# Second attention: the 48 maxima of a step spread over its slots by a build-time table

## The chip, the cores and the metric

The kernel runs on one core of one Trainium2 chip. The core has a tensor engine (PE in the profile, with PEld for its weight loads), a vector engine (DVE), a scalar engine (ACT), a GpSimd engine (POOL) and a sync engine that issues DMAs (SP). The metric is the device time of one execution in microseconds (us); lower is better. Several runs are taken, and the median is compared. One more execution is profiled.

## The reference, cut to what matters

The kernel computes a layer of two residual blocks on `x` of shape (4, 1024, 256): an attention with 16 heads of 64, then a transformer block that holds a second, grouped attention and a mixture of experts. The change lies in the second attention alone, which has 16 query heads and 4 key-value heads of 16 columns:

```
scores = jnp.einsum('bqhd,bkhd->bhqk', q, k) * scale
scores = jnp.where(causal[None, None], scores, jnp.finfo(scores.dtype).min)
probs = jax.nn.softmax(scores, axis=-1)
attn = jnp.einsum('bqhk,bkhd->bqhd', probs, v)
```

(The last line stands for the product of the probabilities with the values.) The softmax takes the maximum of each row first. It is these maxima that the change moves.

## The kernel before, in words

`attention_two` (line 1103) goes through 16 tasks, one for each of 4 batches and 4 key-value heads, with 4 query heads each. Its `run` (line 1141) makes a pipeline of them: `step(n1, n2, n3)` prepares task n1 (stacks and maxima), computes scores, exponentials and outputs of task n2, and brings out the second half of task n3. So there are 16 steps with work on n1, then two more that drain.

Every engine goes through the same `NU2` = 48 slots `k` of a step, and the program writes down in each slot what that engine does there; nothing is reordered later. A slot has one unit of scores: `UNITS2[k]` is (c, j, h), queries of half c (512 of them), key tile j of 128, head h. Below the diagonal all 512 columns are computed, on it fewer. Slots 0 to 15 are c = 0 with 512, 384, 256 and 128 columns, four slots each; slots 16 to 35 have 512 columns, 36 to 47 again 384, 256 and 128.

In a slot PE does, in this order (`step`, lines 1390 to 1437): the scores of slot k (line 1332); at each fourth slot, for the two units that trail from the task before, an output group of four heads (line 1346); in slots 0, 3, 8, 12 and 16 a stack (line 1370), eight transposes that bring the keys or one head's queries into a PSUM bank; the maxima of the slot (line 1381); at each fourth slot, later ones, the output group; and in a few slots the turns: `turn_minus` (line 1387) transposes the negated maxima of a half, and `turn_out` (line 1352) the outputs. "Output group u" below is that of unit u of the current task; group 0 stands in slot 11, group 1 in slot 15, and so on every four slots up to group 9 in slot 47. The last two units of a task come in slots 3 and 7 of the next step.

A max is a matmul of 128 queries against up to 512 keys into one of three shared banks `b_MX`, which DVE then reduces to one column of `b_peak`. `MAX2[u]` says which. Where the key block holds the diagonal, `reduce_max` (line 1271) adds the causal mask and takes the maximum in one masked operation of 128 to 512 columns followed by a reading of its accumulator (line 1279); else it is a plain reduction of 512 columns (line 1282). Maxima 0 to 15 are all masked, with 128, 256, 384 and 512 columns in turn, four per head; they make the first half. From 16 on plain and masked ones alternate. Behind max 15 and max 47 DVE takes the negated maximum of the half (line 1288); PE transposes it, DVE splits it (lines 1296, 1298), and two DMAs of SP put it into two rows of `b_Q`, which scores 0 and 16 wait for.

Before the change max u stands in slot u + 6, one in every slot, so that maxima 42 to 47 ("late") fall into slots 0 to 5 of the next step, while the next task's stacks begin there. Max 4h, the first of head h, also waits for ACT's copies of the stacks (lines 1238, 1240) it reads. `share_banks` (line 1076) gives stacks, maxima and late maxima their banks in the order of the program: before, the stacks of slots 0, 8, 12 and 16 are in bank 0, that of slot 3 in bank 2, maxima 0 to 13 alternate between banks 1 and 2, and from 14 on they go round all three. A matmul into a bank waits until the last user has been read (`bank_free`).

Scores go round three banks of their own, `b_SC`: score k waits for the exponential of score k - 3 on ACT (line 1229). POOL zeroes the upper triangle of the probabilities (line 1171).

Of the kernel before, what the change touches and what calls it, by code (L numbers as in the profile page):

```python
# [16 lines left out]
P = 128  # L17
BANK = 512
# [19 lines left out]
def first_col(c, j):  # L38

    return max(0, j * P - c * BANK)  # L40
# [727 lines left out]
def project_two(nc, x, hold, w_qkv, ln1, cos2, sin2, norm_z, shift_z, V2, stack_dram):  # L768
# [3 lines left out]
    with ExitStack() as ctx:  # L772
# [251 lines left out]
        def _(pe):  # L1024
# [31 lines left out]
UNITS2 = [(c, j, h) for c, j in UNITS for h in range(GROUP)]  # L1056
NU2 = len(UNITS2)
MAX2 = [(h, i, c) for first in (True, False) for h in range(GROUP) for i, c in MAXU if (i < BANK // P) == first]
# [4 lines left out]
MAX_START = 6  # L1063
TAKE2 = (24, 8)
HALF_MAX = (16, NU2)
TURN_SLOTS = (MAX_START + 20, MAX_START + 3)
SCORE_BANKS, MAX_BANKS = 3, 3
OUT_SLOTS = (16 + LAG2 + 5, LAG2 + 3)
MAX_AT = {k: [n for n in range(NU2) if n + MAX_START == k] for k in range(MAX_START + NU2)}


SHARED = [x for k in range(NU2) for x in [("stack", n) for n, at in enumerate(STACK_SLOTS) if at == k]
          + [("max", u) for u in MAX_AT.get(k, ())] + [("late", u) for u in MAX_AT.get(k + NU2, ())]]

# [17 lines left out]
def used_so_far(n1, n2, x):  # L1092

    bank = SHARED_BANK[x]
    mine = [y[0] for y in SHARED[:SHARED.index(x)] if SHARED_BANK[y] == bank]
    if n2 is None:
        return LATE_USES[bank] + len(mine) - mine.count("late")
    if n1 is None:
        return (n2 + 1) * SHARED_USES[bank] + mine.count("late")
    return n1 * SHARED_USES[bank] + len(mine)  # L1100


def attention_two(nc, stack_dram, V2, A2):

    with ExitStack() as ctx:
# [141 lines left out]
        @block.vector  # L1247
        def _(dve):
            dve.memset(peak[:, :, :, :], 3 * NEG).then_inc(s["dve_consts"], 1)
            for i in range(2):  # L1250
                dve.memset(K[i][STACK:, :], 1.0).then_inc(s["dve_consts"], 1)
            dve.wait_ge(s["dve_consts"], 3)
            dve.wait_ge(s["consts"], 6)
            for b in range(MAX_BANKS):
                dve.sem_inc(bank_used[b], LATE_USES[b])
            dve.sem_inc(s["turn_copied"], 1)
            for c in range(2):
                dve.sem_inc(minus_in[c], 1)
            dve.sem_inc(s["A2_done"], 1)

            def rows_out(n2, c):
                b, g = n2 // KV2, n2 % KV2
                dve.wait_ge(s["OT_ready"], n2 * 2 + c + 3)
                O4 = SM[:, :].rearrange("p (t h w) -> p t h w", t=4, h=GROUP)
                dve.reciprocal(inv[:, c, :, :], O4[:, :, :, DH2]).then_inc(s["inv_ready"], 1)
                dve.wait_ge(s["inv_ready"], n2 * 2 + c + 1)
                dve.tensor_tensor(A2[:, bass.ds(b * ST_N + 4 * c, 4), bass.ds(g * (GROUP * DH2), GROUP * DH2)].rearrange(
                    "p t (h d) -> p t h d", h=GROUP), O4[:, :, :, 0:DH2],
                    inv[:, c, :, :].rearrange("p t (h a) -> p t h a", a=1).to_broadcast([P, 4, GROUP, DH2]), ALU.mult).then_inc(s["A2_done"], 1)

            def reduce_max(n, u, n1, n2, x):
                h, i, ch = MAX2[u]
                w = min(BANK, (i + 1) * P - ch * BANK)
                bank = SHARED_BANK[x]
                dve.wait_ge(s["max_ready"], n * NU2 + u + 1)
                if ch == i * P // BANK:

                    dve.sem_inc(s["due"], 1)
                    dve.tensor_tensor_reduce(MX[bank][:, 0:w], MX[bank][:, 0:w], causal[:, BANK - w:], 1.0, 3 * NEG,  # L1279
                                             ALU.add, ALU.max, peak[:, h, i, ch:ch + 1]).then_inc(bank_used[bank], 1)  # L1280
                else:
                    dve.tensor_reduce(peak[:, h, i, ch:ch + 1], MX[bank][:, 0:w], AX.X, ALU.max).then_inc(bank_used[bank], 1)  # L1282
                for c in range(2):
                    if u == HALF_MAX[c] - 1:
                        for b in range(MAX_BANKS):
                            y = [y for y in SHARED[:SHARED.index(x) + 1] if SHARED_BANK[y] == b and y[0] == x[0]][-1]
                            dve.wait_ge(bank_used[b], used_so_far(n1, n2, y) + 1)
                        dve.tensor_reduce(minus[c][:, :, :], peak[:, :, 4 * c:4 * c + 4, :], AX.X, ALU.max,
                                          negate=True).then_inc(s["minus_ready"], 1)

            def turn(n, c):
                dve.wait_ge(s["turn_ready"], n * 2 + c + 1)

                dve.wait_ge(minus_in[c], n * 32 + 1)
                T = SM[0:GROUP * ST_N // 2, 0:P]
                dve.tensor_copy(hi[c][:, :], T).then_inc(s["turn_copied"], 1)
                dve.wait_ge(s["turn_copied"], n * 4 + 2 * c + 2)
                dve.tensor_tensor(lo[c][:, :], T, hi[c][:, :], ALU.subtract).then_inc(s["turn_copied"], 1)

            def step(n1, n2, n3, p):  # L1300
                for k in range(NU2):
                    for c, m in ((0, n2), (1, n3)):
                        if m is not None and k == OUT_SLOTS[c] + 2:
                            rows_out(m, c)
                    for u in MAX_AT[k]:
                        if n1 is not None:
                            reduce_max(n1, u, n1, n2, ("max", u))
                    for u in MAX_AT.get(k + NU2, ()):
                        if n2 is not None:
                            reduce_max(n2, u, n1, n2, ("late", u))  # L1310
                    for c, m in ((0, n1), (1, n2)):
                        if m is not None and k == TURN_SLOTS[c]:
                            turn(m, c)

            run(dve, step)

        @block.tensor
        def _(pe):
# [71 lines left out]
            def step(n1, n2, n3, p):  # L1390
                for k in range(NU2):
                    unit = k // GROUP - TRAIL
                    last_head = k % GROUP == GROUP - 1
                    if n2 is not None and k > 0:
                        scores(n2, 1 - p, k)
                    if n3 is not None and last_head and unit < 0:
                        output(n3, p, NU + unit)
                    if n1 is not None and k in STACK_SLOTS:
                        n = STACK_SLOTS.index(k)
                        if n == 0:  # L1400
                            pe.wait_ge(loaded[p], (n1 - p) * 72 + 144)
                        stack(n1, n2, p, n)
                    for u in MAX_AT[k]:
                        if n1 is not None:
                            maximum(n1, p, u, n1, n2, ("max", u))
                    for u in MAX_AT.get(k + NU2, ()):
                        if n2 is not None:
                            maximum(n2, 1 - p, u, n1, n2, ("late", u))
                    if n2 is not None and k == 0:

                        scores(n2, 1 - p, 0)
                    if n2 is not None and last_head and unit >= 0:
                        output(n2, 1 - p, unit)
                    if n2 is not None and k == TURN_SLOTS[1]:
                        if n3 is not None:
                            rows_done(n3, 0)
                        else:
                            turned(n2, 0)
                        turn_minus(n2, 1)
                    if n3 is not None and k == OUT_SLOTS[1]:  # L1420
                        if n2 is not None:
                            turned(n2, 1)
                        else:
                            rows_done(n3, 0)
                        turn_out(n3, 1)
                    if n1 is not None and k == TURN_SLOTS[0]:
                        if n3 is not None:
                            rows_done(n3, 1)
                        elif n2 is not None:
                            turned(n2, 1)  # L1430
                        turn_minus(n1, 0)
                    if n2 is not None and k == OUT_SLOTS[0]:
                        if n1 is not None:
                            turned(n1, 0)
                        else:
                            rows_done(n3, 1)
                        turn_out(n2, 0)
# [773 lines left out]
```

## Time and profile before

| | us |
|---|---|
| median of 3 runs | 2751.97 |
| lowest and highest | 2751.84, 2753.37 |
| the profiled execution | 2745.91 |
| its span, first to last instruction | 2744.2 |
| PE busy | 2388.5 (87%) |
| DVE busy | 1636.8 (60%) |
| ACT busy | 1446.1 (53%) |
| POOL busy | 965.5 (35%) |

The span is one execution's; the profiled execution's own time is 1.7 us longer than it. Busy times count each engine's instructions alone. Matmuls are pipelined, so that the durations of neighbours overlap: the distance from start to start says what a matmul costs the next. The mean granted clock of PE over the span is 0.945 of full speed.

### The profile page before, as it was taken

What the parts mean: (1) busy time and instruction counts of PE and PEld (TensorE: products, weight loads), DVE (VectorE), ACT (ScalarE), POOL (GpSimd) and SP (SyncE); (2) the same over time, 40 slices, a digit from 0 to 9 for tenths busy, and PEclk for the clock granted to TensorE, in tenths of its full rate; (3) what the DMA queues carried; (4) which work ended last, traced back from release to release, by engine and by line L of the source; (5) the groups of instructions that cost most, each with busy time, mean ns of one, the idle gap of its engine ahead of it and who ended that gap; (6) DMA issues with size and microseconds to landing.
All of it is one profiled execution on the core that took longest, in us unless ns stands there. A gap on an engine that the chain in (4) does not pass through costs nothing. (4 is left out here: it accounts for less than half of the span.)

```text
span 2744.2 us, 45471 instructions
## 1 busy us (share of the span) xinstructions
PE 2388.5 (87%) x12594; PEld 1372.3 (50%) x12595; DVE 1636.8 (60%) x4291; ACT 1446.1 (53%) x3189; POOL 965.5 (35%) x1727
## 2 busy tenths in 40 slices
PE   4999999999999999999735899999998749999980
PEld 2555566555665556555512333333334626666650
DVE  5676664776467773676188777777773452222227
ACT  3566654666456663665257477777775412222222
POOL 0344433444345542444326122222222033333323
PEclk8999999999999999999968799999999869999995
DMA  3011110101001110111124111111111611111114
GB/s 103 17 28 29 25 44 15 29 22 41 24 19 29 29 44 14 29 26 28 32 97 194 40 35 34 35 35 35 35 34 58 218 51 44 46 44 46 46 55 163
DMA packets 134983, 135.01 MB, mean 49 GB/s; under 512 B 67840, under 2 KB 104448, under 8 KB 133120
## 3 DMA queue, kind: packets, MB, share of 16 engines
q1 hardware_dynamic: 125760, 109.58, 13.4%
q0 software_dynamic: 6912, 18.88, 2.1%
q10 hardware_dynamic: 2112, 4.19, 0.4%
q8 instruction: 88, 1.44, 0.2%
q14 instruction: 111, 0.91, 0.1%
HBM read 87.50 MB, written 33.82 MB: 44 GB/s over the span
## 5 line engine op out<-in xcount | busy, mean ns | idle before, releaser
L288 POOL TENSOR_TENSOR a_A<-a_A,a_P 128x512 f32<-128x512 f32 (+3 forms) x320 | 316.5, 989 | 289.8 <-PE a_O L594 279.0
L1229 ACT ACTIVATE b_P<-b_SC 128x512 f32<-128x512 f32 (+3 forms) x768 | 328.8, 497 | 163.0 <-PE b_SC L1332 161.4
L442 ACT ACTIVATE a_P<-a_SC 128x512 f32<-128x512 f32 (+3 forms) x640 | 292.0, 469 | 201.2 <-PE a_SC L577 194.9
L500 DVE CUSTOM_DVE_ANT_0 a_MX<-a_MX,a_causal 128x128 f32<-128x128 f32 (+3 forms) x512 | 248.5, 501 | 154.8 <-PE a_MX L646 149.3
L576 PE MATMUL a_SC<-a_QR,a_KR 128*128 128x512 f32 (+3 forms) x768 | 317.3, 417 | 4.6 <-DMA a_QS<-a_minusT 2.9
L1171 POOL TENSOR_SCALAR_AFFINE_SELECT b_P<-b_P 128x128 f32<-128x128 f32 x512 | 147.0, 294 | 443.0 <-ACT b_P L1229 433.6
L646 PE MATMUL a_MX<-a_KR,a_QR 128*128 128x512 f32 (+3 forms) x768 | 282.6, 377 | 17.5 <-DVE a_peak L500 14.3
L1279 DVE CUSTOM_DVE_ANT_0 b_MX<-b_MX,b_causal 128x128 f32<-128x128 f32 (+3 forms) x512 | 248.5, 498 | 80.3 <-PE b_MX L1381 78.1
L1381 PE MATMUL b_MX<-b_K,b_Q 96*128 96x512 bf16 (+3 forms) x768 | 251.7, 339 | 42.3 <-ACT b_Q L1240 14.0
L577 PE MATMUL a_SC<-a_QS,a_KS 65*128 65x512 f32 (+3 forms) x768 | 264.5, 348 | 0.0
L327 POOL TENSOR_SCALAR_AFFINE_SELECT a_P<-a_P 128x128 f32<-128x128 f32 x448 | 144.8, 329 | 339.7 <-ACT a_P L442 336.3
L1955 PE MATMUL e_GU<-W,e_hT 128*128 x576 | 261.8, 597 | 1.0 <-ACT e_hT L2007 0.8
L1332 PE MATMUL b_SC<-b_Q,b_K 98*128 98x512 bf16 (+3 forms) x768 | 245.5, 330 | 3.5 <-ACT b_P L1229 1.5
L594 PE MATMUL a_O<-a_P,a_V 128*64 128x512 f32 (+3 forms) x1280 | 232.6, 476 | 3.8 <-POOL a_P L327 3.8
L503 DVE TENSOR_REDUCE a_peak<-a_MX 128x1 f32<-128x512 f32 x256 | 169.7, 684 | 94.2 <-PE a_MX L646 94.1
L288 DVE TENSOR_TENSOR a_A<-a_A,a_P 128x512 f32<-128x512 f32 (+3 forms) x320 | 212.5, 664 | 16.6 <-PE a_O L594 6.1
L576 PEld LDWEIGHTS a_SC<-a_QR,a_KR 128*128 128x128 f32 x768 | 145.0, 189 | 148.1 <-issue 69.0
L1282 DVE TENSOR_REDUCE b_peak<-b_MX 128x1 f32<-128x512 f32 x256 | 176.0, 687 | 41.4 <-PE b_MX L1381 40.4
L620 PE MATMUL a_PK<-hold,a_W 128*128 128x512 f32 x384 | 187.2, 611 | 10.1 <-DMA a_W<-in_w_pair 6.8
L646 PEld LDWEIGHTS a_MX<-a_KR,a_QR 128*128 128x128 f32 x768 | 145.7, 190 | 85.8 <-DVE a_peak L500 55.3
L2047 DVE TENSOR_TENSOR e_gate<-e_gate,e_GU 128x512 f32<-128x512 f32 x72 | 49.5, 688 | 208.2 <-PE e_GU L1955 208.2
L1346 PE MATMUL b_O<-b_P,b_V 128*32 128x512 f32 (+3 forms) x1536 | 163.4, 498 | 0.2
(258 smaller groups left out, 4083.5 us busy)
## 6 DMA issues: line engine op xcount, KB each, us to landing
a_inv<-inv_rows SPq DMA_DIRECT2D x128, 128.0 KB, 3.1
stack_rows<-p_stk SPq DMA_DIRECT2D x32, 480.0 KB, 2.7
a_W<-in_w_pair SPq DMA_DIRECT2D x34, 384.0 KB, 3.9
b_stk<-stack_rows SPq DMA_DIRECT2D x136, 96.0 KB, 2.1
W<-in_w SPq DMA_DIRECT2D x8, 1024.0 KB, 5.5
n_x<-in_x SPq DMA_DIRECT2D x4, 1024.0 KB, 9.5
a_xT<-hold SPq DMA_DIRECT2D x4, 1024.0 KB, 4.9
a_fold<-a_total SPq DMA_DIRECT2D x256, 1.0 KB, 2.0
```

The costliest lines, as they stand in the source:

```text
L288: eng.tensor_tensor(acc[h][c][:, a:], acc[h][c][:, a:], buffer(n, h)[:, a:], ALU.add).then_inc(added[h], 1)
L442: act.activation(buffer(n, h)[:, a:], SC[h][:, a:], ACT.Exp, scale=DH1 ** -0.5).then_inc(s["exp_done"], 1)
L500: dve.tensor_tensor_reduce(MX[c % MAX_BANKS1][:, 0:w], MX[c % MAX_BANKS1][:, 0:w], causal[:, BANK - w:], 1.0, 3 * NEG, ALU.add, ALU.max, p ...
L576: pe.matmul(SC[h][:, a:], KR[p][h][:, keys], QR[p][h][:, queries], start=True, stop=False)
L577: pe.matmul(SC[h][:, a:], KS[p][h][:, keys], QS[p][h][:, queries], start=False, stop=True).then_inc(s["scores_ready"], 1)
L594: pe.matmul(O[DH1 * h:DH1 * (h + 1), a:], V[p][h][:, j, :], buffer(n, h)[:, a:], start=(j == 0), stop=(n in LAST)).then_inc(s["pv_done"], 1)
L646: pe.matmul(bank[:, 0:w], QR[p][h][:, i * P:(i + 1) * P], KR[p][h][:, ch * BANK:ch * BANK + w], start=True, stop=True).then_inc(s["max_rea ...
L1229: act.activation(probs[k % RING2][:, a:], SC[k % SCORE_BANKS][:, a:], ACT.Exp, scale=DH2 ** -0.5).then_inc(s["exp_done"], 1)
L1279: dve.tensor_tensor_reduce(MX[bank][:, 0:w], MX[bank][:, 0:w], causal[:, BANK - w:], 1.0, 3 * NEG, ALU.add, ALU.max, peak[:, h, i, ch:ch + ...
L1332: pe.matmul(SC[k % SCORE_BANKS][:, a:], K[p2][:, j * P:(j + 1) * P], Q[p2][:, c, h, a:], start=True, stop=True).then_inc(s["scores_ready"], 1)
L1381: last = pe.matmul(MX[SHARED_BANK[x]][:, 0:w], Q[p][0:STACK, i // 4, h, i % 4 * P:(i % 4 + 1) * P], K[p][0:STACK, ch * BANK:ch * BANK + w] ...
L1955: last = pe.matmul(GU[i][half][:, :], hT[i][:, kt, :], W13[:, bass.ds(e, 1), kt, half * FFN:(half + 1) * FFN].rearrange("p a f -> p (a f)" ...
```

## The change

`MAX_AT`, the table from slots to maxima, is no longer "max u in slot u + 6". `spread_maxima` gives each slot of PE a weight, its score columns + 300, and each max one for DVE, its columns + 150, and puts each next max into the first slot at which PE's share of the step has reached DVE's share of the maxima so far. The result, written out:

- slots with two maxima: 1 (43, 44), 6 (0, 1), 18 (12, 13), 22 (17, 18), 29 (25, 26), 31 (27, 28)
- slots with none: 5, 13, 30, 42, 44, 46
- in all others one, in the same order: max 2 in slot 7, max 8 in 14, max 19 in 23, max 29 in 32, max 37 in 40, max 41 in 47, max 47 in 4.

`TURN_SLOTS` is computed from the table and becomes (25, 8) instead of (26, 9). `share_banks` runs over the new order: the stacks of slots 0, 3 and 16 are now in bank 0, those of 8 and 12 in bank 1, and the late maxima alternate between 1 and 2. The rest of the diff lets the code cope with a slot without maxima and a bank without late ones.

```diff
--- before.py
+++ after.py
@@ -1063,10 +1063,28 @@
 MAX_START = 6
 TAKE2 = (24, 8)
 HALF_MAX = (16, NU2)
-TURN_SLOTS = (MAX_START + 20, MAX_START + 3)
 SCORE_BANKS, MAX_BANKS = 3, 3
 OUT_SLOTS = (16 + LAG2 + 5, LAG2 + 3)
-MAX_AT = {k: [n for n in range(NU2) if n + MAX_START == k] for k in range(MAX_START + NU2)}
+
+
+
+def spread_maxima():
+
+    pe = [BANK - first_col(c, j) + SLOT_COST for c, j, h in UNITS2]
+    dve = [(BANK if ch != i * P // BANK else (i + 1) * P - ch * BANK) + MAX_COST for h, i, ch in MAX2]
+    at, done, k = {}, 0, MAX_START
+    for u in range(NU2):
+        while sum(pe[m % NU2] for m in range(MAX_START, k + 1)) / sum(pe) < done / sum(dve):
+            k += 1
+        at.setdefault(k, []).append(u)
+        done += dve[u]
+    return at
+
+
+SLOT_COST, MAX_COST = 300, 150
+MAX_AT = spread_maxima()
+MAX_SLOT2 = {u: k for k, us in MAX_AT.items() for u in us}
+TURN_SLOTS = (MAX_SLOT2[HALF_MAX[0] - 1] + 5, MAX_SLOT2[NU2 - 1] + 4 - NU2)
 
 
 SHARED = [x for k in range(NU2) for x in [("stack", n) for n, at in enumerate(STACK_SLOTS) if at == k]
@@ -1252,7 +1270,8 @@
             dve.wait_ge(s["dve_consts"], 3)
             dve.wait_ge(s["consts"], 6)
             for b in range(MAX_BANKS):
-                dve.sem_inc(bank_used[b], LATE_USES[b])
+                if LATE_USES[b]:
+                    dve.sem_inc(bank_used[b], LATE_USES[b])
             dve.sem_inc(s["turn_copied"], 1)
             for c in range(2):
                 dve.sem_inc(minus_in[c], 1)
@@ -1283,8 +1302,9 @@
                 for c in range(2):
                     if u == HALF_MAX[c] - 1:
                         for b in range(MAX_BANKS):
-                            y = [y for y in SHARED[:SHARED.index(x) + 1] if SHARED_BANK[y] == b and y[0] == x[0]][-1]
-                            dve.wait_ge(bank_used[b], used_so_far(n1, n2, y) + 1)
+                            here = [y for y in SHARED if SHARED_BANK[y] == b]
+                            done = [y for y in here if y[0] == x[0] and SHARED.index(y) <= SHARED.index(x)]
+                            dve.wait_ge(bank_used[b], used_so_far(n1, n2, done[-1]) + 1 if done else used_so_far(n1, n2, here[0]))
                         dve.tensor_reduce(minus[c][:, :, :], peak[:, :, 4 * c:4 * c + 4, :], AX.X, ALU.max,
                                           negate=True).then_inc(s["minus_ready"], 1)
 
@@ -1302,7 +1322,7 @@
                     for c, m in ((0, n2), (1, n3)):
                         if m is not None and k == OUT_SLOTS[c] + 2:
                             rows_out(m, c)
-                    for u in MAX_AT[k]:
+                    for u in MAX_AT.get(k, ()):
                         if n1 is not None:
                             reduce_max(n1, u, n1, n2, ("max", u))
                     for u in MAX_AT.get(k + NU2, ()):
@@ -1400,7 +1420,7 @@
                         if n == 0:
                             pe.wait_ge(loaded[p], (n1 - p) * 72 + 144)
                         stack(n1, n2, p, n)
-                    for u in MAX_AT[k]:
+                    for u in MAX_AT.get(k, ()):
                         if n1 is not None:
                             maximum(n1, p, u, n1, n2, ("max", u))
                     for u in MAX_AT.get(k + NU2, ()):
```

Line numbers move by 20: scores are line 1352 in the changed kernel, outputs 1366, `turn_out` 1372, stacks 1390, maxima 1401, `turn_minus` 1407. The names are those of the banks and tiles: `b_SC` a score, `b_MX` a max or a stack, `b_O` an output group.

PE's instructions in slots 20 to 25 of a step with work on all three tasks, from max 15 to max 19. Before:

```order
L1381 MATMUL b_MX<-b_K,b_Q 128x512
L1332 MATMUL b_SC<-b_Q,b_K 128x512
L1381 MATMUL b_MX<-b_K,b_Q 128x512
L1332 MATMUL b_SC<-b_Q,b_K 128x512
L1381 MATMUL b_MX<-b_K,b_Q 128x128
L1346 MATMUL b_O<-b_P,b_V 32x128 x4
L1332 MATMUL b_SC<-b_Q,b_K 128x512
L1381 MATMUL b_MX<-b_K,b_Q 128x512
L1332 MATMUL b_SC<-b_Q,b_K 128x512
L1381 MATMUL b_MX<-b_K,b_Q 128x256
```

and now:

```order
L1401 MATMUL b_MX<-b_K,b_Q 128x512
L1352 MATMUL b_SC<-b_Q,b_K 128x512
L1401 MATMUL b_MX<-b_K,b_Q 128x512
L1352 MATMUL b_SC<-b_Q,b_K 128x512
L1401 MATMUL b_MX<-b_K,b_Q 128x128
L1401 MATMUL b_MX<-b_K,b_Q 128x512
L1352 MATMUL b_SC<-b_Q,b_K 128x512
L1401 MATMUL b_MX<-b_K,b_Q 128x256
L1366 MATMUL b_O<-b_P,b_V 32x128 x4
```

Max 18 (512 columns) now follows max 17 (128) at once, and max 19 (256) stands ahead of the output group (`b_O`) instead of two scores behind it.

PE's instructions in slots 10 to 12, from max 4 on. Before:

```order
L1381 MATMUL b_MX<-b_K,b_Q 128x128
L1332 MATMUL b_SC<-b_Q,b_K 128x256
L1381 MATMUL b_MX<-b_K,b_Q 128x256
L1346 MATMUL b_O<-b_P,b_V 32x512 x4
L1332 MATMUL b_SC<-b_Q,b_K 128x128
L1370 MATMUL b_MX<-b_identb,b_stk 96x128 x8
L1381 MATMUL b_MX<-b_K,b_Q 128x384
```

and now, from slot 9:

```order
L1401 MATMUL b_MX<-b_K,b_Q 128x128
L1352 MATMUL b_SC<-b_Q,b_K 128x256
L1401 MATMUL b_MX<-b_K,b_Q 128x256
L1352 MATMUL b_SC<-b_Q,b_K 128x256
L1401 MATMUL b_MX<-b_K,b_Q 128x384
L1366 MATMUL b_O<-b_P,b_V 32x512 x4
L1352 MATMUL b_SC<-b_Q,b_K 128x128
L1390 MATMUL b_MX<-b_identb,b_stk 96x128 x8
L1401 MATMUL b_MX<-b_K,b_Q 128x512
```

Max 6 (384 columns) has come in front of the output group, and behind the stack now stands max 7 (512).

PE's instructions in slots 44 to 47 and the first of the next step. Before:

```order
L1332 MATMUL b_SC<-b_Q,b_K 128x128
L1381 MATMUL b_MX<-b_K,b_Q 128x512
L1332 MATMUL b_SC<-b_Q,b_K 128x128
L1381 MATMUL b_MX<-b_K,b_Q 128x512
L1332 MATMUL b_SC<-b_Q,b_K 128x128
L1381 MATMUL b_MX<-b_K,b_Q 128x512
L1332 MATMUL b_SC<-b_Q,b_K 128x128
L1381 MATMUL b_MX<-b_K,b_Q 128x128
L1346 MATMUL b_O<-b_P,b_V 32x384 x4
L1370 MATMUL b_MX<-b_identb,b_stk 96x128 x8
```

and now:

```order
L1352 MATMUL b_SC<-b_Q,b_K 128x128 x2
L1401 MATMUL b_MX<-b_K,b_Q 128x512
L1352 MATMUL b_SC<-b_Q,b_K 128x128 x2
L1401 MATMUL b_MX<-b_K,b_Q 128x128
L1366 MATMUL b_O<-b_P,b_V 32x384 x4
L1390 MATMUL b_MX<-b_identb,b_stk 96x128 x8
```

Two maxima have left these four slots, so that scores follow each other in pairs, and the stack of the next step's slot 0 comes behind two maxima instead of four.

## Rows read from the trace of the kernel before

**Rows 1.** One line's instructions: duration ns min/median/max, first and last start us, forms.

```profile
L1381 PE MATMUL b_MX<-b_K,b_Q x768: 216/379/634, 1515.2 to 2074.5; 96*128 96x512 bf16 x128, 96*128 96x128 bf16 x64
```

**Rows 2.** Timeline of PE at late max 42: start us, us, instruction.

```profile
1541.56 0.63 PE L1381 MATMUL b_MX<-b_K,b_Q 96*128 96x512 bf16 x1
...
2071.01 0.39 PE L1381 MATMUL b_MX<-b_K,b_Q 96*128 96x512 bf16 x1
```

**Rows 3.** Windows: stretch: us, busy of each engine, granted clock, DMA share, GB/s.

```profile
1542.70:1577.95 35.25, 31.80 (x221) 12.93 (x220) 26.81 (x88) 25.22 (x54) 9.22 (x32) 0.95 0.13 33
...
1613.18:1648.41 35.23, 32.22 (x245) 13.16 (x244) 27.77 (x90) 25.64 (x55) 9.23 (x32) 1.00 0.13 34
```

**Rows 4.** Waits of PE's loads, 1577.8 to 2107: total us, times, longest.

```profile
PEld b_MX L1381 <- DVE b_peak L1282: 38.6, 99, 1.0
...
PEld b_MX L1381 <- ACT b_Q L1240: 26.3, 42, 0.8
```

**Rows 5.** Timeline of PE through one step: start, us, instruction, idle before.

```profile
1613.18 0.38 PE L1381 MATMUL b_MX<-b_K,b_Q 96*128 96x512 bf16 x1
1613.40 0.60 PE L1332 MATMUL b_SC<-b_Q,b_K 98*128 98x512 bf16 x2
...
1614.35 0.39 PE L1381 MATMUL b_MX<-b_K,b_Q 96*128 96x512 bf16 x1
...
1614.88 0.64 PE L1346 MATMUL b_O<-b_P,b_V 128*32 128x256 f32 x8
...
1617.79 0.22 PE L1381 MATMUL b_MX<-b_K,b_Q 96*128 96x128 bf16 x1
...
1618.99 0.61 PE L1370 MATMUL b_MX<-b_identb,b_stk 128*96 128x128 bf16 x8
...
1620.75 0.22 PE L1381 MATMUL b_MX<-b_K,b_Q 96*128 96x128 bf16 x1 [0.37 <-ACT b_Q L1240]
...
1621.49 1.07 PE L1346 MATMUL b_O<-b_P,b_V 128*32 128x512 f32 x8
1622.49 0.23 PE L1332 MATMUL b_SC<-b_Q,b_K 98*128 98x128 bf16 x1
...
1628.37 0.28 PE L1381 MATMUL b_MX<-b_K,b_Q 96*128 96x256 bf16 x1
...
1630.79 0.43 PE L1346 MATMUL b_O<-b_P,b_V 128*32 128x128 f32 x8
...
1632.11 0.28 PE L1381 MATMUL b_MX<-b_K,b_Q 96*128 96x256 bf16 x1
...
1643.90 0.34 PE L1381 MATMUL b_MX<-b_K,b_Q 96*128 96x384 bf16 x1
...
1646.40 0.23 PE L1381 MATMUL b_MX<-b_K,b_Q 96*128 96x128 bf16 x1 [0.18 <-DVE b_peak L1282]
...
1647.96 0.62 PE L1370 MATMUL b_MX<-b_identb,b_stk 128*96 128x128 bf16 x8 [0.55 <-DVE b_peak L1279]
```

**Rows 6.** Timeline of DVE in the same step: maxima 42, 47, 0, 16 and 17.

```profile
1613.60 0.69 DVE L1282 TENSOR_REDUCE b_peak<-b_MX 128x1 f32<-128x512 f32 x1 [1.02 <-PE b_MX L1381]
...
1617.72 0.70 DVE L1279 CUSTOM_DVE_ANT_0 b_MX<-b_MX,b_causal 128x512 f32<-128x512 f32 x1
1618.33 0.14 DVE L1279 DVE_READ_ACCUMULATOR2_ANT b_peak<- 128x1 f32 x1
...
1618.67 0.30 DVE L1279 CUSTOM_DVE_ANT_0 b_MX<-b_MX,b_causal 128x128 f32<-128x128 f32 x1
...
1631.38 0.68 DVE L1282 TENSOR_REDUCE b_peak<-b_MX 128x1 f32<-128x512 f32 x1
1631.97 0.29 DVE L1279 CUSTOM_DVE_ANT_0 b_MX<-b_MX,b_causal 128x128 f32<-128x128 f32 x1
```

**Rows 7.** Timeline of PE, four scores of the last step.

```profile
2095.36 0.34 PE L1332 MATMUL b_SC<-b_Q,b_K 98*128 98x128 bf16 x3
2095.96 0.23 PE L1332 MATMUL b_SC<-b_Q,b_K 98*128 98x128 bf16 x1 [0.26 <-ACT b_P L1229]
```

## The prediction

> **What bounds the kernel now.** I read the page's groups first, then the table by windows, the waits, and last the timelines of PE, DVE and ACT through one step. The change touches only the second attention, whose max matmuls lie between 1515 and 2075 us [rows 1]. From late max 42 of its second step to that of its last [rows 2] are 529.5 us for 15 steps, 35.3 us each; the one used below is 35.23 us long. In it PE is busy 32.2 us, DVE 27.8, ACT 25.6 and POOL 9.2, all at full granted clock [rows 3]. PE is the busiest and so the one whose gaps count; the waits put them down to a bank that DVE has not read yet, or to ACT's copies [rows 4].
>
> PE's "busy" overlaps, so I take start to start. T is the start of late max 42, 1613.18 [rows 5]. A matmul of 512 columns is followed 0.22 us later by the next, and narrower ones in proportion (0.17, 0.11, 0.06). An output group of four heads takes 1.00 at 512 columns, and 0.78, 0.57 and 0.36 for the narrower ones elsewhere in the same timeline; each starts 0.10 late. 48 scores and 48 maxima have the same columns in all, 15.9 us; 12 output groups are 10.6, stacks and turns 3.5: 30.0 us of work. The other 5.2 us per step are stalls. The change can win at most these, and it moves them.
>
> The stalls that matter stand at three places [rows 5]. Early: max 4 at T+7.57, which waits for ACT's copy of the stack begun at T+5.81 (1.76 later). Middle: max 13 at T+15.19, which waits for the bank of max 11, and max 19 at T+18.93 for that of max 16. End: max 37 (0.29), max 41 (0.34), and the next step's stack 0 (0.62), since the last eight slots give DVE 8 maxima while PE has little else.
>
> **What one wait costs.** A plain reduction starts 0.42 us after its matmul, ends 0.69 later, and max 44 has the bank 0.06 after that; where work is ready, the next one starts 0.59 after it [rows 5, 6]. The masked ones are ready 0.43 to 0.52 after theirs up to 384 columns, by the same timeline. The masked form of 512 columns starts 0.57 after its matmul and frees the bank 0.81 after its start (0.61 to the reading of the accumulator, 0.14 for that, 0.06); one of 128 columns frees it after 0.41. The last max of a half has the negated maximum behind it: the next operation starts 0.95 after it, not 0.61.
>
> **The change, part by part.** Nothing is added or removed: the same matmuls, reductions and DMAs run. 48 maxima stand in other slots, two in slots 1, 6, 18, 22, 29 and 31, none in 5, 13, 30, 42, 44 and 46; stacks and late maxima change banks; the two turns stand one slot earlier. I follow PE through one step with these durations and say at each output group how far it is behind the old time, less the maxima it has done more.
>
> A, slots 0 to 11. Max 44 may start at T+1.17 as before, but score 2 is now behind it: the output group of slot 3 goes from T+1.70 to 2.15, with one max of 0.17 more done, +0.28. Max 0 waits for the same copy of ACT, T+4.61. Max 1 now follows at 4.99, when DVE has freed 47's bank; stack 2 goes from 5.81 to 6.01, max 4 with it from 7.57 to 7.77. Max 6 now stands ahead of output group 0, in the bank of max 4, which is free at 7.77 + 0.43 + 0.42 = 8.62. Group 0 starts at 8.89 instead of 8.31 with 0.17 more done: **+0.41**. The stall of max 9 (0.41 before) is then covered: **-0.27**.
>
> B, slot 18. Max 13 waits for max 11 as before (1.46 after it, 15.33), but score 19 is now behind it and no longer covers the wait: **+0.21**.
>
> C, slots 21 to 23. Max 15 starts at 16.71. DVE reads it from 17.28; its bank comes free at 18.09, and max 18, now in slot 22, waits for that bank (0.44). Behind the negated maximum, max 16 is read from 18.24 and free at 18.99, and max 19 waits for that. So max 19 starts at 18.99 against 18.93, nearly the same time; but before it PE had by then done output group 3, score 24 and score 25 (0.9 us), and now it has not. Output group 3 starts at 19.20 against 17.61, 0.33 more done: **+0.91**. Before, max 19 itself cost 0.29 after that group; this goes: **-0.30**.
>
> D, slots 29 to 39. Maxima 27, 28, 34, 35 and 36 each miss their bank by 0.05 to 0.23, where before there is no stall: **+0.40**. Bounds: nothing, or 0.6.
>
> E, slots 40 to 47 and the next stack 0. Five maxima stand there instead of eight: their banks are free, and DVE is done 0.6 earlier. The three stalls (1.25) fall to about 0.3. In their place comes a wait for one of the three score banks: in the last step, which has no maxima between scores, the fourth score of a group waits 0.26 for an exponential [rows 7], and scores 43 and 47 now do so in part (0.08 and 0.2, within the 0.3). **-0.94**.
>
> Sum: 0.41 - 0.27 + 0.21 + 0.91 - 0.30 + 0.40 - 0.94 = **+0.42 us a step**. 15 steps give 6.3. In the last half step no max 0 follows, and max 47 loses its wait: -0.3. The first step has no scores, and its maxima run at DVE's pace, whatever slot they stand in; I take 0 there (bounds -1 and +1). In all **+6.0 us**.
>
> I cost the two turns at nothing. Their DMAs start a slot earlier, and between a turn and the first score that needs its row lie 4 us of PE's work or more (slots 9 to 16, and 26 to 48); without that cover score 16 would wait for the row.
>
> One rule would change the sum. A 512-column matmul is followed 0.22 us later, max 42 by the scores for one [rows 5]. The Trainium skill, TensorE: Matmul & The Clock Gate, section Back-to-back issue gap, gives about 131 ns for a sustained stream of loads and matmuls of 512 columns. By it the 48 such matmuls of a step would need 4.3 us less, PE's work would be less than DVE's 27.8 us, and the sum would be near 0. That would be the time of the second rival below; the row contradicts the rule, so it gets no chance of its own and the sum goes by the row.
>
> **How it stands to the runs.** The sum is against the profiled execution, 2745.91 us, so 2751.9 for such a one; the median of the runs, 2751.97, lies 6.1 above it, and with 6.0 more it becomes **2758.0 us**.
>
> **The rivals.** What can be told from no change here is about 0.2%, 5.5 us.
>
> 1. Slower, as worked out: +6 (bounds of its own 2754 to 2764, from 0.15 to 0.8 us a step). Chance 0.42.
>
> 2. No change to speak of. If the small misses of D are not there, since a release that is 0.05 earlier is enough, a step gains 0.4 back and the sum is 0; 2752, from 2747 to 2757. For it: D rests on differences smaller than the spread of DVE's starts. Chance 0.33.
>
> 3. Faster: the first half costs nothing. The place is output group 0 and max 1: if ACT's copy of stack 2 starts at its old time, since it waits for the exponentials of slots 4 to 8 in any case, max 4 keeps T+7.57, and if max 6 finds its bank, A is 0; with D at 0 too the step is at -0.4, and 15 steps give 6 us: 2746. It decides from A and D together below 0.4. If C is half as large as well, it is -0.85 a step, 2739. Against it: max 19 cannot start before DVE has read max 16, and that order is fixed. Chance 0.20.
>
> 4. The clock. In the first of the 15 steps the granted clock is 0.95, and it is 36.3 us long instead of 35.23 [rows 2, 3]. If the stalls before output group 3, now 0.9 us in a row with only short work between them, made the clock fall once in some steps, each would cost up to 1.1 us; in 8 of 15 that is 9 us beside the 6: 2767. Against it: the stalls of up to 0.6 us today leave it at 1.00. Chance 0.05. The Trainium skill, same page, section A second HAM failure mode: psum-queue depth-cycling, says that cycling through PSUM banks lets PE idle shortly between groups until its clock swings between its two levels; by that rule a kernel with such waits would already show it, and the windows do not.
>
> That the change does nothing is excluded: the order of the instructions on PE and DVE is another one in every step.
>
> **How the numbers follow.** Slower by over 0.2%: 0.42 and 0.05, 0.47. Within: 0.33. Faster: 0.20. The range takes rivals 1 and 2 whole and the nearer parts of 3 and 4: 2744 to 2766.
>
> **What the new profile would show.** Right: steps of about 35.65 us; max 18 and max 19 each waiting for DVE, with output group 3 at about T+19.2; max 6 waiting some 0.4 us ahead of group 0; no wait of maxima 37 and 41; stack 0 of the next step without its 0.6 us; DVE's busy time as before. Wrong: max 19 at T+18.5 or earlier, or a step under 35.2 us.

## The result, and the profile after

| | before | after |
|---|---|---|
| median (20 runs each) | 2751.62 | 2758.94 |
| lowest to highest | 2742.97 to 2753.37 | 2751.01 to 2763.44 |
| the profiled execution | 2745.91 | 2757.03 |
| its span | 2744.2 | 2755.3 |
| PE / DVE / ACT / POOL busy | 2388.5 / 1636.8 / 1446.1 / 965.5 | 2392.4 / 1639.4 / 1446.9 / 961.5 |
| mean granted clock of PE | 0.945 | 0.944 |

The ratio of the times is 1.0033, with a 95% interval of 1.0025 to 1.0040: slower by about 9 us (7 to 11). The means of the runs differ by 8.7 us, the two medians by 7.3; most runs of before lie near 2752 and some near 2743, so that its median says less than the ratio. The forecast was slower, 2758.0 us, by 6.0 us.

The two traces, cut at the stage's own marks, show where it went. The marks are the first stack, late max 42 of the second step, the same of the last step [rows 2], and the start of the last output groups.

| stretch | before | after | difference | forecast |
|---|---|---|---|---|
| first step: stacks and maxima alone | 29.56 | 32.05 | +2.49 | 0 |
| 15 steps | 529.45 | 535.61 | +6.16 | +6.3 |
| last half step | 25.11 | 25.53 | +0.42 | -0.3 |
| sum | 584.12 | 593.19 | +9.07 | +6.0 |

So in these two profiles the second attention alone accounts for the 9 us of the runs. The two profiled executions differ by 2 us more; that lies behind the stage, where the program is the same.

The windows of the changed kernel, one steady step from late max 42 to late max 42 (us, busy time and instructions of PE, PEld, DVE, ACT, POOL; granted clock, DMA share, GB/s), against the second of [rows 3]:

```profile
1615.84:1651.47 35.63, 32.25 (x245) 12.50 (x244) 28.01 (x90) 25.72 (x55) 9.08 (x32) 1.00 0.13 33
```

35.63 us (forecast 35.65), busy times within 0.7 us of the old ones, the clock still at 1.00. Only waits have changed. The timeline of PE in this step, T = 1615.84, against [rows 5]:

```profile
1617.98 0.64 PE L1366 MATMUL b_O<-b_P,b_V 128*32 128x256 f32 x8
...
1620.45 0.22 PE L1401 MATMUL b_MX<-b_K,b_Q 96*128 96x128 bf16 x1 [0.32 <-ACT b_Q L1258]
1620.87 0.28 PE L1401 MATMUL b_MX<-b_K,b_Q 96*128 96x256 bf16 x1 [0.20 <-DVE b_peak L1298]
...
1623.65 0.22 PE L1401 MATMUL b_MX<-b_K,b_Q 96*128 96x128 bf16 x1 [0.71 <-ACT b_Q L1258]
...
1624.47 0.34 PE L1401 MATMUL b_MX<-b_K,b_Q 96*128 96x384 bf16 x1 [0.27 <-DVE b_peak L1298]
1624.74 1.07 PE L1366 MATMUL b_O<-b_P,b_V 128*32 128x512 f32 x8
...
1631.20 0.28 PE L1401 MATMUL b_MX<-b_K,b_Q 96*128 96x256 bf16 x1 [0.28 <-DVE b_peak L1298]
...
1633.97 0.39 PE L1401 MATMUL b_MX<-b_K,b_Q 96*128 96x512 bf16 x1 [0.29 <-DVE b_peak L1298]
1634.86 0.28 PE L1401 MATMUL b_MX<-b_K,b_Q 96*128 96x256 bf16 x1 [0.28 <-DVE b_peak L1301]
1635.07 0.43 PE L1366 MATMUL b_O<-b_P,b_V 128*32 128x128 f32 x8
...
1643.59 1.07 PE L1366 MATMUL b_O<-b_P,b_V 128*32 128x512 f32 x8
```

In this order, with the place that the prediction had worked out in brackets: the output group of slot 3 at T+2.14 (2.15); max 0, 4.61 (4.61); max 1, 5.03 (4.99); max 4, 7.81 (7.77); max 6, 8.63 (8.62); output group 0, 8.90 (8.89); max 13, 15.36 (15.33); max 18, 18.13 (18.09); max 19, 19.02 (18.99); output group 3, 19.23 (19.20). For output group 6, at 27.75, the prediction gives no place. Max 18 and max 19 both wait for DVE, as forecast, and the two waits of the old step's end [rows 5], max 41 and stack 0, are gone. These places were right within 0.04 us; what was missed stands outside the steady steps. Of the 15 steps the first is an exception: from stack 0 to stack 0 it takes 36.40 us, less than the 36.72 of before, since the clock is back at 1.00 somewhat sooner; a second profile of before, told below, has 36.11.

### The profile page after: what moved, and what is told of

Its sections match the earlier page's. It is cut to its first block and busy times, and to the rows that moved or that the text cites. A ratio compares the mean times of both kernels' runs of the same rounds, so it can differ in the third digit from the quotient of the medians.

```text
span 2755.3 us, 45469 instructions
## 1 busy us (share of the span) xinstructions
PE 2392.4 (87%) x12594; PEld 1364.8 (50%) x12595; DVE 1639.4 (60%) x4291; ACT 1446.9 (53%) x3189; POOL 961.5 (35%) x1727
## 5 line engine op out<-in xcount | busy, mean ns | idle before, releaser
L1352 PE MATMUL b_SC<-b_Q,b_K 98*128 98x512 bf16 (+3 forms) x768 | 236.1, 330 | 2.9 <-ACT b_P L1247 1.5
```

The lines of the kernel that those rows point to most:

```text
L1352: pe.matmul(SC[k % SCORE_BANKS][:, a:], K[p2][:, j * P:(j + 1) * P], Q[p2][:, c, h, a:], start=True, stop=True).then_inc(s["scores_ready"], 1)
```

## The experiments

The theory: a step's length is set by the bank waits, and each can be worked out from the rows, by which work of PE stands between a max and the one that had its bank. "The walk" below is that working, slot by slot. `share_banks` runs over each new table: for C by itself and for max 13 alone it gives exactly before's banks, for the tail undone exactly the changed kernel's, and for the head undone before's. The rivals are told with each run. Every kernel computes the full result. Medians of the kernel before on the same chip: 2748.5 for the first four runs, 2751.0 for the next four, 2747.6 for the last two; the differences are from the ratios, rounded.

### The negated maximum behind max 16

```diff
-                    if u == HALF_MAX[c] - 1:
+                    if u == (HALF_MAX[0], HALF_MAX[1] - 1)[c]:
+                        last = ("max", HALF_MAX[0] - 1) if c == 0 else x
```

(the waits follow `last` in place of `x`.)

> The changed kernel, with the negated maximum of the first half taken behind max 16 on DVE instead of ahead of it. Theory (max 19 waits for max 16, and max 16 is read late because the negated maximum stands before it): the 0.35 us of that operation leave the path once a step, max 19 starts at about T+18.65 instead of 19.02, steps of 35.28 us instead of 35.63, 5 us less in all. Rival (the step is bound by ACT's copies of the stacks or by PE's own work, and the wait of max 19 only takes up slack): steps stay at 35.6 and the time within 1 us of the changed kernel's.

Measured: 2751.03 us, ratio 1.0012 (1.0001 to 1.0023), 3 us over before where the change is 9 over it. 15 steps take 529.82 us, 5.8 less than with the change; a steady one takes 35.31 from stack 0 to stack 0, 0.33 less, and the rest lies mostly in the first with scores (35.73 against 36.40). PE's timeline (T = 1611.77), max 18, max 19 and output group 3:

```profile
1629.91 0.39 PE L1402 MATMUL b_MX<-b_K,b_Q 96*128 96x512 bf16 x1 [0.29 <-DVE b_peak L1298]
...
1630.45 0.28 PE L1402 MATMUL b_MX<-b_K,b_Q 96*128 96x256 bf16 x1
1630.67 0.43 PE L1367 MATMUL b_O<-b_P,b_V 128*32 128x128 f32 x8
```

Max 19 no longer waits and starts at T+18.68 instead of 19.02. The order on DVE behind max 15 is a real part of C, and moving one reduction of 0.19 us back by one max takes 0.33 of the 0.41 us that a steady step had lost.

### C by itself

Before's table with maxima 17 and 18 beside 16 in slot 22, and 19 in 23, all others at u + 6 (long line broken here).

```diff
-MAX_AT = spread_maxima()
+SLOT_OF = (6, 7, 8, 9, 10, 11, 12, 13, 14, 15, 16, 17, 18, 19, 20, 21, 22, 22, 22, 23, 26, 27, 28, 29,
+           30, 31, 32, 33, 34, 35, 36, 37, 38, 39, 40, 41, 42, 43, 44, 45, 46, 47, 48, 49, 50, 51, 52, 53)
+MAX_AT = {k: [u for u in range(NU2) if SLOT_OF[u] == k] for k in set(SLOT_OF)}
```

> The table of the kernel before (max u in slot u + 6) with one part of the change alone: maxima 17 and 18 in slot 22, max 19 in slot 23, all others in their old slots. Theory (two or three maxima moved ahead of an output group lose the cover that group and two scores gave to their waits): output group 3 starts 0.9 to 1.3 us later with 0.33 us of maxima done more, and nothing later gives it back: +0.6 to +1.0 us a step, 9 to 15 us in all, more than the whole change costs. Rival (the lateness is taken up by the stalls at the end of the step, since DVE has idle time): within 2 us of the kernel before.

Measured: 2766.94 us, ratio 1.0070 (1.0053 to 1.0088), 19 us (15 to 24) over before. 15 steps take 544.36, 36.29 each: +0.99 a step, 14.9 in all. T = 1613.09:

```profile
1631.14 0.39 PE L1402 MATMUL b_MX<-b_K,b_Q 96*128 96x512 bf16 x1 [0.42 <-DVE b_peak L1299]
...
1632.03 0.28 PE L1402 MATMUL b_MX<-b_K,b_Q 96*128 96x256 bf16 x1 [0.28 <-DVE b_peak L1302]
1632.24 0.43 PE L1367 MATMUL b_O<-b_P,b_V 128*32 128x128 f32 x8
```

The same pair of waits as in the changed kernel, and output group 3 at T+19.15. Three maxima moved by one or two slots cost more than the whole change.

### Stack 1 in another bank, twice

Banks 0 and 2 are exchanged from stack 1 on (a line behind `share_banks`'s loop), so that stack 1 need not wait for the reader of stack 0.

```diff
+    for x in [("stack", 1), ("late", 47)] + SHARED[SHARED.index(("max", 1)):]:
+        bank[x] = (2, 1, 0)[bank[x]]
```

> The changed kernel with banks 0 and 2 exchanged from stack 1 and max 47 on, so that stack 1 no longer goes into the bank of stack 0. Theory (the first step is 2.5 us longer than before partly because PE must wait for ACT's copy of stack 0 before it can bring in stack 1, and there is nothing else to do there): the first max starts about 1.1 us earlier after the first stack, steps as in the changed kernel, 35.6; 1.1 us less in all. Rival (the longer first step comes from the order of maxima and stacks alone): no difference there.

Measured: 2761.83 us, ratio 1.0054 (1.0038 to 1.0070). The first step fell by 1.33, from 32.05 to 30.72, as expected. But the whole was no faster. A steady step is 35.79 from stack 0 to stack 0 where the changed kernel has 35.64 (max 1 at T+5.18, not 5.03), 2 us in all; and the first step with scores took 40.69 us from stack 0 (1546.87) to stack 0 (1587.56), against 36.40 in the changed kernel. The windows of this run show why:

```profile
1559.00:1561.00 2.00, 1.96 (x9) 0.31 (x9) 1.05 (x4) 0.38 (x1) 0.59 (x2) 0.50 0.06 12
1561.00:1563.00 2.00, 2.00 (x16) 1.24 (x12) 0.00 (x0) 0.76 (x2) 0.29 (x1) 0.53 0.29 88
1563.00:1565.00 2.00, 1.44 (x14) 0.48 (x13) 1.59 (x6) 1.15 (x4) 0.82 (x3) 1.00 0.73 201
```

and those of the changed kernel, whose stack 0 stands at 1543.06:

```profile
1545.00:1547.00 2.00, 2.00 (x6) 0.57 (x5) 1.31 (x4) 1.99 (x4) 0.29 (x1) 0.50 0.01 4
1547.00:1549.00 2.00, 1.79 (x14) 1.03 (x13) 1.51 (x4) 2.00 (x5) 0.88 (x3) 0.89 0.00 0
```

The granted clock stays at 0.50, 1.2 GHz, until some 16 us behind stack 0, where the changed kernel has it back at 2.4 GHz some 4 us behind. The kernel of the first experiment and the one with the tail undone, below, have the banks and the first slots of the changed kernel, and in both the clock is back within 5 us of stack 0. To tell chance from cause the kernel with the exchange ran again.

> The kernel of the run with banks 0 and 2 exchanged from stack 1 on, once more. Its first step with scores was 40.7 us from stack 0 to stack 0, since the granted clock stayed at 0.50 until 1562.9 us, 15.9 us behind its second stack 0, where the changed kernel had it back 4 us behind. If the late return of the clock belongs to the exchange, this profile shows it again, and a time of 2760 us or more; if it is chance, the clock is back within 5 us of stack 0 in about this one, and the time is near 2757.

Measured: 2762.17 us, ratio 1.0047 (1.0031 to 1.0063); stack 0 at 1545.90, the next at 1586.60, 40.70 us; the clock was 0.50 up to 1560 and 0.81 on average from there to 1565. It repeats, and the start of the stage does not decide it: with the tail undone the first stack stands at 1516.78, here at 1517.00 and 1516.03. The 15 steps of the first of these profiles took 541.19 us, 5.6 more than the changed kernel's, against the 1.3 saved. That the exchange brings it about is shown by the two profiles with it and the three without; by what in PE's work is not.

### Max u in slot u + 7

> Max u in slot u + 7, one in every slot, in place of u + 6. Theory (what a step costs is set by which maxima and which PE work stand between a max and the one three before it in its bank, whatever the number of maxima in a slot): a walk through the step with the rows' durations gives a step 1.0 us shorter than before's, about 34.2 us, so about 15 us less than before, with max 0 no longer waiting for stack 1's copy and the wait for max 19 staying at 0.3. Rival (what counts is that every slot has one maximum, so only the tables with pairs and empty slots lose): no change, within 3 us of before.

Measured: 2740.74 us, ratio 0.9958 (0.9943 to 0.9974), about 12 us less than before. A step is 34.37 us (1615.51 to 1649.88), 0.86 less than the 35.23 between the same stacks of before. The walk gave 34.2, and 15 us less in all. The rival, that one max in every slot is what counts, falls: the same even spread one slot later wins more than the change cost.

### Max 13 alone in slot 18

> Before's table with max 13 alone moved from slot 19 to slot 18, the prediction's step B by itself. Theory: max 13 still waits for the bank of max 11, score 19 no longer covers that wait: +0.2 us a step, steps of about 35.45, +3 us in all. Rival (the wait is covered later, by output group 2 and the score behind it): steps as before, 35.23, and no difference.

Measured: a step is 35.46 us (1613.98 to 1649.44), +0.23 against before's 35.23 [rows 3], and max 13 waits 0.28 for DVE at T+15.2 (T = 1614.43). The run times can't show it: 2751.49 us, ratio 1.0009 (0.9998 to 1.0020), 2.5 us with an interval that holds both the theory and the rival. The trace decides for +0.2.

### The tail undone

The changed table with maxima 37 to 41 in slots 43 to 47.

> The changed table with maxima 37 to 41 put back to slots 43 to 47, the prediction's step E undone and all else kept. Theory: the gain of E, 0.94 us a step, is given back: the waits of max 41 (0.35) and of the next step's stack 0 (0.5) are there again, steps of about 36.5 us against 35.6, about 14 us more than the changed kernel and 23 more than before. Rival (the end of the step is set by the scores' banks and ACT, not by the maxima): steps stay at 35.6, and the time is that of the changed kernel.

Measured: 2772.15 us, ratio 1.0085 (1.0069 to 1.0102), 23 us over before and 14 over the change. A step is 36.73 us from 1622.50 to 1659.23, with both old waits at its end:

```profile
1657.67 0.23 PE L1402 MATMUL b_MX<-b_K,b_Q 96*128 96x128 bf16 x1 [0.17 <-DVE b_peak L1302]
1657.83 0.85 PE L1367 MATMUL b_O<-b_P,b_V 128*32 128x384 f32 x8
1659.23 0.62 PE L1391 MATMUL b_MX<-b_identb,b_stk 128*96 128x128 bf16 x8 [0.55 <-DVE b_peak L1299]
```

E's gain is real and a little larger than forecast: 1.09 a step between stacks, not 0.94. They are the waits of [rows 5] at 1646.40 and 1647.96 again.

### The head undone

The changed table with maxima 0 to 11 and 42 to 47 back at u + 6.

> The changed table with maxima 0 to 11 and the late ones 42 to 47 back in before's slots (u + 6), the prediction's step A undone and all else kept. Theory: a step gives back A's +0.14 net, steps of about 35.45 against 35.63, and the first step gives back most of its 2.5, since max 3 stands behind stack 2 again and stack 1 is in a bank of its own again: about 30 us from the first stack to the first late max against 32.05. Together 4 to 5 us less than the changed kernel. Rival (the first step's 2.5 is chance, set by the clock or by when the stage begins): the first step stays at 32, and only about 2 us are gained.

Measured: 2751.71 us, ratio 1.0015 (1.0005 to 1.0025), 4 us over before, 5 less than the change. A step is 35.48 us (1609.22 to 1644.70), and the first step 29.59 (1508.61 to 1538.20): the whole 2.5 of the first step is gone, so the first step's loss comes from the head of the table and its banks, not from chance. The expectation names max 3 as the one that changed sides with stack 2; it is max 2, as the rows of the next section show.

### Before, once more

> The kernel before once more, for a second profile. Its runs lie in two groups, near 2743 and near 2752. If the spread lies outside the second attention, this profile has the same 29.6 us first step and the same 529.5 us for 15 steps as the first one, whatever its own time; if it lies inside (when the clock comes back in the first step with scores), the 15 steps differ by several us.

Measured: 2751.66 us (2743.63 to 2752.21), ratio 1.0002; the profiled execution 2751.91. Its first step is 29.57 us (1517.09 to 1546.66), its 15 steps 528.95 (to 2075.61), against 29.56 and 529.45 in the first profile. But the stage begins at 1517.09 instead of 1512.00. Most of the 6 us between the two executions lies ahead of the second attention, and no difference told above rests on it, since all are taken from the stage's first stack on.

### Another table, found with the walk

Since the walk had given the changed step nearly exactly, a table was sought by which it gives a short step (long line broken here):

```diff
-MAX_AT = spread_maxima()
+SLOT_OF = (8, 10, 10, 11, 11, 12, 13, 15, 16, 16, 19, 19, 19, 20, 21, 21,
+           23, 25, 25, 27, 27, 28, 29, 30, 31, 32, 32, 32, 34, 36, 36, 39, 39, 41,
+           42, 42, 44, 46, 48, 50, 50, 51, 51, 52, 53, 54, 54, 54)
+MAX_AT = {k: [u for u in range(NU2) if SLOT_OF[u] == k] for k in set(SLOT_OF)}
```

> The changed kernel with another table of slots, written down from the same walk through a step: maxima ahead of a copy or of a late bank are put behind the work that covers them, and in groups of two or three directly before or after an output group (slots 8 10 10 11 11 12 13 15 16 16 19 19 19 20 21 21 23 25 25 27 27 28 29 30 31 32 32 32 34 36 36 39 39 41 42 42 44 46 48 50 50 51 51 52 53 54 54 54 for maxima 0 to 47). Theory (PE's stalls are waits without cover, and the place of a max against the output groups decides): stalls fall from 6 us to about 2.5 a step, steps of 32.4 to 33.2 us, 30 to 42 us less than before the change. Rival (DVE with 28 us busy in 35 and its late starts is what bounds, or PE's clock falls when maxima come in clusters): steps not below 34.5.

Measured: 2716.83 us, ratio 0.9878 (0.9859 to 0.9898): 33 us less than before, faster than both kernels. A step is 32.79 us from stack 0 to stack 0 (expected: 32.4 to 33.2). The waits of PE in it, 1614 to 1647 (total us, times, longest):

```profile
PE b_MX L1402 <- DVE b_peak L1299: 0.6, 2, 0.4
PE b_MX L1391 <- DVE b_peak L1299: 0.2, 1, 0.2
PE b_MX L1402 <- DVE b_peak L1302: 0.2, 1, 0.2
```

and of the changed kernel from 1615.84 to 1651.47:

```profile
PE b_MX L1401 <- ACT b_Q L1258: 1.4, 3, 0.7
PE b_MX L1401 <- DVE b_peak L1298: 1.0, 4, 0.3
PE b_MX L1401 <- DVE b_peak L1301: 0.5, 2, 0.3
PE b_MX L1401 <- issue: 0.4, 1, 0.4
```

3.3 us of waits have become 1.0. The waits for ACT's copies are gone: maxima 0, 4, 8 and 12 stand in slots 8, 11, 16 and 19, farther behind their stacks (slots 3, 8, 12, 16) than in slots 6, 9, 14 and 18. This table has pairs, triples and empty slots too, so an uneven table is not in itself what costs. What wins is not taken apart here: most of its maxima stand later than in the changed kernel as well, and one slot later for all was by itself worth 0.86 us a step.

## Why the prediction was right, and where it was off

**The steps** were right: +0.41 a step measured, +0.42 forecast, with the places and the waits as forecast. A and B were tried by themselves, with max 13 alone (+0.23; 0.21 forecast) and the head undone (-0.16 between stacks; 0.14 forecast, A's net). C came to +0.99 alone, where its terms inside the change are 0.91 - 0.30 = 0.61: within the 0.6 to 1.0 expected. The two are not the same edit: in the change maxima 14 to 16 stand one slot earlier as well, so that DVE is done with them earlier against PE's work, and alone they do not; that this makes the difference was not tried. E is 1.09 by the tail undone, 0.94 forecast. D, the small misses, was not tried by itself, but the timeline of the steady step shows it:

```profile
1639.73 0.65 PE L1401 MATMUL b_MX<-b_K,b_Q 96*128 96x256 bf16 x2
1640.31 1.07 PE L1366 MATMUL b_O<-b_P,b_V 128*32 128x512 f32 x8
...
1644.82 0.33 PE L1352 MATMUL b_SC<-b_Q,b_K 98*128 98x384 bf16 x1
1645.05 0.39 PE L1401 MATMUL b_MX<-b_K,b_Q 96*128 96x512 bf16 x1
1645.28 0.33 PE L1352 MATMUL b_SC<-b_Q,b_K 98*128 98x384 bf16 x1
1645.60 0.28 PE L1401 MATMUL b_MX<-b_K,b_Q 96*128 96x256 bf16 x1
```

Maxima 27 and 28 and the output group behind them take 0.58 where their columns need 0.43 (0.11, 0.22 and 0.10); max 34 comes 0.23 and max 35 0.32 behind a score of 384 columns that takes 0.17. That is 0.15, 0.06 and 0.15, in all 0.36 against the 0.40 of the sum, in three maxima (28, 34, 35) where five were named; 27 and 36 do not wait. The total was right, part of its make-up by luck. The second rival, no change because D is absent, falls with these rows, and the third, faster because A is, with those of the first half: max 4 did not keep T+7.57 and group 0 stood at 8.90.

That the median came out at 2758.94 beside the 2758.0 named is closer than the working was: the change cost 9 us and not 6, and two terms outside the steps missed 3 us in the same direction.

**The first step** was the mis-sized term: "I take 0 there (bounds -1 and +1)", and it was +2.5, outside the bounds. "Its maxima run at DVE's pace, whatever slot they stand in" was the step that failed. PE's timeline there, at half clock; before:

```profile
1512.00 1.94 PE L1370 MATMUL b_MX<-b_identb,b_stk 128*96 128x128 bf16 x16 [18.97 <-DMA b_stk<-stack_rows]
1515.15 0.48 PE L1381 MATMUL b_MX<-b_K,b_Q 96*128 96x128 bf16 x2 [1.21 <-issue]
1515.43 1.06 PE L1370 MATMUL b_MX<-b_identb,b_stk 128*96 128x128 bf16 x8
...
1517.77 0.27 PE L1381 MATMUL b_MX<-b_K,b_Q 96*128 96x128 bf16 x1 [0.53 <-DVE b_peak L1279]
```

and after:

```profile
1511.86 1.09 PE L1390 MATMUL b_MX<-b_identb,b_stk 128*96 128x128 bf16 x8 [19.67 <-DMA b_stk<-stack_rows]
1514.06 1.09 PE L1390 MATMUL b_MX<-b_identb,b_stk 128*96 128x128 bf16 x8 [1.11 <-ACT b_K L1256]
1516.30 0.80 PE L1401 MATMUL b_MX<-b_K,b_Q 96*128 96x128 bf16 x3 [1.16 <-ACT b_Q L1258]
1517.22 1.09 PE L1390 MATMUL b_MX<-b_identb,b_stk 128*96 128x128 bf16 x8
...
1519.47 0.67 PE L1401 MATMUL b_MX<-b_K,b_Q 96*128 96x128 bf16 x2 [0.73 <-ACT b_Q L1258]
```

Before, stacks 0 and 1 lie in banks 0 and 2 and follow each other (x16). Now both are in bank 0, and stack 1 waits 1.11 us for ACT to copy stack 0. In a steady step the slots between them cover that; the first step has nothing there. The second part is the order: max 2 stands ahead of stack 2 instead of behind it (x3 ahead of it in place of x2). Stack 2 comes 5.36 us behind the first stack instead of 3.43, and max 4 follows it after some 2.3 us in both kernels (1517.77 before, 1519.47 after), so the delay is passed on. The exchange of banks took 1.33 of the 2.5 away, the head undone all of it. I had said of the banks only that they change, and asked of no stage without cover what that does.

**The last half step** was -0.3 in the forecast and +0.4 in the trace. The turns were costed at nothing, with "4 us of PE's work or more" as cover. The last step has no maxima between its scores, and there the cover is thinner: before, score 16 came 3.24 us behind the turn and did not wait; after, it does.

```profile
2084.51 0.27 PE L1407 MATMUL b_SM<-b_ident,b_minus 128*16 128x128 f32 x1 [0.21 <-DVE b_minus L1308]
...
2085.30 1.07 PE L1366 MATMUL b_O<-b_P,b_V 128*32 128x512 f32 x8 [0.19 <-ACT b_OT L1239]
...
2088.37 0.82 PE L1352 MATMUL b_SC<-b_Q,b_K 98*128 98x512 bf16 x3 [0.45 <-DMA b_Q<-b_lo]
```

The DMA issues of that stretch say that the two rows took 1.6 and 1.7 us to land before, 2.4 and 2.3 after. The earlier turn is not the reason for that. The kernel with the exchanged banks has the changed kernel's turns, its rows took 1.6 and 1.7, score 16 did not wait (3.46 us behind the turn), and the stretch is 25.01 us in both of its profiles. C by itself has the turns in before's slots, and its rows took 2.4 and 2.3 and score 16 waited 0.66. What goes along with the slow rows is one packet of the DMA queue for instructions (q8), which stands in this stretch in every kernel, but not at the same place: 4.9 us ahead of the first row's packets before, 2.0 with the exchanged banks, 0.7 in the changed kernel and 0.9 with C by itself. In all four profiles in which it stands under 1 us ahead (the other two are the negated maximum behind max 16 and the tail undone) the rows took 2.3 us or more, in the other eight 1.6 and 1.7. No run moved that packet alone, so that it slows the rows is not shown. Without the 0.45 the stretch would be at about 0, not at -0.3: max 44 waits 0.24 there, a part of A that the forecast had not counted in it.

**The rule on the issue gap** (the Trainium skill, TensorE: Matmul & The Clock Gate, Back-to-back issue gap) would have given a sum near 0. The steps are 35.63 us, and in the timeline after, too, a max of 512 columns is followed 0.22 us later (max 44 at 1617.01, score 2 at 1617.23); the row was the right one to take. **The clock rival** falls too: ahead of output group 3 PE loses 0.9 us from start to start, as forecast, and the granted clock from 1549 to 2080 us is 1.00 throughout.

## What to carry to other kernels

Where three users share banks, cost a moved instruction by what stands between it and the bank's last user, not by how evenly the table spreads the work: max, DVE's reading and release take 1.2 to 1.4 us here for 512 columns, and where PE has less work than that between the two, it waits for the rest. In the pipeline's first and last step part of the work is missing, and waits that the steady step hides come out (here 1.3 us for one bank); walk those two steps too, with the bank table in hand. And once such a walk agrees with the trace, it can be used to choose the table: here a proportional rule lost 9 us, and a table chosen by the walk won 33.

## What the runs showed of the hardware that I had not expected

The clock's return in the first step with scores depends on the order of the instructions before it, and repeats. PE runs at 0.50 (1.2 GHz) through the first step, whose maxima leave it waiting for DVE. With the change 1.00 is back about 4 us behind the next stack 0; with banks 0 and 2 exchanged about 16 us behind, in both profiles of that kernel, for some 4 us of time. It does not take an exchange of banks: the fastest table has it back only some 12 us behind, and its first step with scores takes 36.22 us where its steady one takes 32.79. A change of bank can so cost more by the clock than the wait that it removes.
